# An fp32 attention and FFN layer on one core: other places for a few operations at the passage to Q and in front of O, and the low halves of the second half's x blocks moved from GpSimd to VectorE

## Chip, cores and metric

One core of a Trainium2 chip. The metric is the device time of one execution in microseconds; the lower the better.

## What is computed

```python
def reference(x, ctx, mask, Wq, Wk, Wv, Wo, W_base, b_base, W_router, A, B):
    # x, ctx: 16 x 128 x 1024, fp32; 32 query heads, 8 key/value heads of size 128
    q = rope(layernorm(x) @ Wq); k = rope(ctx @ Wk); v = ctx @ Wv
    s = 30 * tanh(q @ k.T * 0.0884 / 30); s = where(mask, s, -1e30)
    x = x + (softmax(s) @ v) @ Wo
    y = layernorm(x)
    w = softmax of the two largest of (y @ W_router.T), 0 for the others
    return x + y @ W_base.T + b_base + 2 * (((y @ A) * w) @ B)
```

## The kernel before

**Precision.** Every fp32 operand z is split in two: a high half (ScalarE copies z to an fp32r tile) and a low half (z less its high half, a subtraction on VectorE or GpSimd). `three` (L233 to L237) makes a product of two split operands from three matmuls, high x high, low x high and high x low, with 512 columns each. The work is in stages: K and V of the context, Q, attention with O, and the FFN.

**Stage Q** goes over 32 turns, 16 pairs of column blocks of Wq for each of two halves of the tokens. A turn n is seven products (Strassen's scheme, in Winograd's form), `QP` (L374), listed as (n, i) in the order i = 0, 1, 4, 3, 2, 5, 6; around turns 14 and 15 they are interleaved so that turn 15 lets go of the first half's x blocks early. The loops count products u = 0 to 223: product 102 is (15, 0), 112 is (16, 0), 113 (16, 1), 115 (16, 3), 117 (16, 5). Each product is 12 matmuls against one of seven x blocks `Xq[i]`. ScalarE (`act_q`) and VectorE (`dve_q`) run the same count. In step u VectorE does, in this order: `q_post` for product u - 1 (it adds products up in PSUM: L994, L998, L1003, L1006, L1009), `q_sum` (sums of Wq parts, L771 to L779), `q_low` of product u + 5 (L877), rope steps of finished turns (`TURN`, L387 to L401, 128x1024 each), and `x_low`, the low halves of an x block (L741). Product (n, 3) needs q_post(n, 1), and product (n, 5) needs q_post(n, 3). In turns 1 to 13 GpSimd does `q_low` for the raw parts of Wq.

**The x blocks of the first half** are loaded at the end of stage K/V. Blocks 5 and 6 are the last, loaded by SyncE when the last V product is done; ScalarE's `x_high` (L731) and VectorE's `x_low` of them stand in steps 1 and 2. **Those of the second half** are made by GpSimd in stage Q (`x_block`, L790): four rounds, round k starting at product XB + XB_STEP k with loads of `Bx`, adds and multiplications in steps 3 to 6 of the round, sums and stores to DRAM up to step 13. `x_load(1, i)` fetches block i once product (15, i) is done, `x_high` follows 4 steps after it, `x_low` in the same step, with the four parts k of a block shared out by `X_POOL` (L965): the listed ones on GpSimd, the others on VectorE. In all 18 parts are GpSimd's (4 + 3 + 3 + 3 + 3 + 2 + 0) and 10 are VectorE's.

**Attention and O** count steps `at` from -16 to 255 (`act_step` L1375, `dve_step` L1453, `pool_step` L1513, `pe_att` L1247). Up to step 0 TensorE still makes V of the last chunk (quarters at -16 to -10, then full products "full0" to "full2" and the last at -8, -6, -4, -2), among them the first scores and values: S0 to S10 stand for score products of the blocks x = 4 gi + b of group gi, PV0 and so on for products with V. For a score block: S on TensorE, tanh on ScalarE (L1387), min with the mask on VectorE (L1485), exp and its high half on ScalarE (L1407, L1409), its low half Pl on VectorE (L1498). For the sums of group gi: a product with ones, its copy `rT` (ScalarE L1401), a load of it into `r16` (GpSimd's queue, L1538), the reciprocal (VectorE L1502), a store to `rD` (L1521) and four loads of `RB` (L1531), both on GpSimd's queue; VectorE multiplies by RB (L1491), ScalarE makes the high half Ah (L1393), VectorE the low half Al (L1465). PV of block x needs Al of block x - 2. `v_high` (L1438), `v_low` (L1444) and `v_store` (GpSimd's queue, L1451, two stores of 256 KB each) take V out of PSUM; PV0 needs v_low(1), full1 needs v_low(0), PV1 needs v_low(4). `w_high` and `w_low` (L1215, L1220) split weights; 8 to 11 are the second half of Wv, which full0 reads, `SPLIT` (L1172) says at which step.

**The order of the work** is written by hand: tables give steps, each engine runs its steps in program order, and waits on semaphores do the rest. `Y` takes up O's products from PSUM: y_add (L1478), from the banks 3, 1, 0 in turn. `f_read` (L1847) says for what an FFN product waits before it writes a bank.

Of the kernel before, what the change touches and what calls it, by code (L numbers as in the profile page):

```python
# [97 lines left out]
def program(nc, xT, xN, ctxT, gran, mask, bias, cst, dram, out):  # L98
    kD, vD, vE, qD, XcD, QSD, X2D, x1D, rD = dram
    ctx = ExitStack()  # L100
    with ctx:
# [677 lines left out]
                e.tensor_tensor(S[:, 3, :], a12, S[:, 1, :], ALU.subtract).then_inc(*t.tick("q_sum", (n, 3)))  # L779


        XB, XB_STEP = 4, 23
        X_PART = {0: (0, 3), 1: (2, 5), 2: (4,), 3: (6, 1)}

        def x_stored(t):
# [176 lines left out]
                m.then_inc(*t.tick("q_pe", (n, i)))  # L962


        X_POOL = {0: (0, 1, 2, 3), 1: (0, 1, 2), 4: (0, 1, 2), 3: (0, 1, 2), 2: (0, 1, 2), 5: (0, 1), 6: ()}  # L965

        def act_q(t):
            e = t.e
            for u in range(NU + 1):
                if 0 < u and QP[u - 1][1] == 0:  # L970
                    n = QP[u - 1][0]
                    t.wait_ge("q_pe", (n, 0))
                    if n > 1:
                        for i in (4, 5, 6):
                            t.wait_ge("q_post", (n - 2, i))
                    e.activation(qp[n % 2][0][:, :], ps[qbank[n % 2][0]][:, :], ACT.Copy).then_inc(*t.tick("q_s1", n))
                if u + AHEAD < NU:
                    q_high(t, u + AHEAD)
                if u in (1, 2):
                    x_high(t, 0, 4 + u)  # L980
                if 0 <= u - 4 < NU and QP[u - 4][0] == 15:
                    x_high(t, 1, QP[u - 4][1])
                act_att_early(t, u)
# [57 lines left out]
        def dve_q(t):  # L1041
            for u in range(NU + 7):
# [6 lines left out]
                for x, ahead, i in ((0, 7, 1), (1, 6, 1), (2, 6, 3), (3, 7, 6)):  # L1049
                    if u + ahead < NU and 0 < QP[u + ahead][0] < 16 and QP[u + ahead][1] == i:  # L1050
                        q_sum(t, QP[u + ahead][0], x)
                if u + AHEAD < NU and not q_by_pool(u + AHEAD):
                    q_low(t, u + AHEAD)
                if u in (1, 2):
                    x_low(t, 0, 4 + u)
                for n, steps in TURN.get(u, []):
# [79 lines left out]
            x.sort()  # L1136
        PL_AT = {}
        for at, gi in DEN_AT.items():
            for b, d in enumerate((1, 2, 2, 2) if gi < 3 else (1, 2, 4, 6)):
                PL_AT.setdefault(at + d, []).append((gi, b))  # L1140
        NT = 8 * NG
        sbank, obank, tbank, ring = [4, 5], [2, 6], 7, [3, 1, 0]
# [232 lines left out]
        def act_step(t, at):  # L1375
            e = t.e
            if at == -16:
                q_high2(t, 0)
                q_high2(t, 1)
            v_high(t, at)  # L1380
            for x in SPLIT.get(at, []):
                w_high(t, x)
            for gi, b in S_AT.get(at, []):
                x = 4 * gi + b
                s = ps[sbank[x % 2]][:, :]
                t.wait_ge("a_s", x)
                e.activation(s, s, ACT.Tanh, scale=SCALE / CAP).then_inc(*t.tick("a_tanh", x))  # L1387
                q_high2(t, x + 2)
# [5 lines left out]
            if at in DEN_AT:  # L1394
                gi = DEN_AT[at]
                t.wait_ge("a_den", gi)
                if gi > 1:
                    t.wait_ge(f"d_rt{gi % 2}", gi - 2)
                else:
                    t.wait_ge("q_pe", (31, 4))  # L1400
                e.activation(rT[gi % 2][:, :], Tb[:, :], ACT.Copy).then_inc(*t.tick("a_rt", gi))  # L1401
            for gi, b in S_AT.get(at, []):
                x = 4 * gi + b
                s = ps[sbank[x % 2]][:, :]
                t.wait_ge("a_min", x)
                p_free(t, x)
                e.activation(Pf[x % NP][:, :], s, ACT.Exp, scale=CAP).then_inc(*t.tick("a_exp", x))  # L1407
                t.wait_ge("a_exp", x)
                e.activation(Ph[x % NP][:, :], Pf[x % NP][:, :], ACT.Copy).then_inc(*t.tick("a_ph", x))  # L1409
# [36 lines left out]
        def v_store(t, at):  # L1446
            for n in V_EVAC.get(at, []):
                half, b4 = n // 4, n % 4
                t.wait_ge("v_vl", n)
                for x in range(2):  # L1450
                    t.e.dma_start(vE[x, b4][:, T * half:T * half + T], f(v_place(n)[:, x, :])).then_inc(*t.tick(f"d_vp{n % 2}{x}", n, 16))  # L1451

        def dve_step(t, at):  # L1453
            e = t.e
            if at == -16:
                q_low2(t, 0)
                q_low2(t, 1)
            v_low(t, at)
            for gi, b in S_AT.get(at - 1, []):
                q_low2(t, 4 * gi + b + 2)  # L1460
            for gi, b in PV_AT.get(at - 1, []):
                x, i = 4 * gi + b, gi % 2
                t.wait_ge("a_ah", x)
# [2 lines left out]
            if at >= 9:  # L1466
# [9 lines left out]
                else:  # L1476
                    t.wait_ge("y_first", m)
                e.tensor_tensor(Y[:, m, :], ps[ring_bank(n)][:, :], Y[:, m, :], ALU.add).then_inc(*t.tick("y_add", n))  # L1478
            for x in [y for y in SPLIT.get(at, []) if at < 0]:
                w_low(t, x)  # L1480
            for gi, b in S_AT.get(at, []):
                x = 4 * gi + b
# [3 lines left out]
            for gi, b in PV_AT.get(at, []):  # L1486
# [2 lines left out]
                t.wait_ge("a_pv", x)  # L1489
                t.wait_ge(f"d_rb{b}", gi)  # L1490
                e.tensor_tensor(o, o, RB[:, b, :], ALU.mult).then_inc(*t.tick("a_an", x))  # L1491
            for x in [y for y in SPLIT.get(at, []) if at >= 0]:
                w_low(t, x)
            for gi, b in PL_AT.get(at, []):
                x = 4 * gi + b
                t.wait_ge("a_ph", x)
                t.wait_ge("a_den", gi)
                e.tensor_tensor(Pl[x % NP][:, :], Pf[x % NP][:, :], f(Ph[x % NP][:, :]), ALU.subtract).then_inc(*t.tick("a_pl", x))  # L1498
            if at - 1 in DEN_AT:
                gi = DEN_AT[at - 1]  # L1500
                t.wait_ge(f"d_rt{gi % 2}", gi)
                e.reciprocal(r16[gi % 2][:, :], r16[gi % 2][:, :]).then_inc(*t.tick("a_rec", gi))  # L1502
            if 11 <= at < 19:
                n = at - 11
                t.wait_ge("y_add", n + 8)
# [6 lines left out]

        def pool_step(t, at):  # L1513
            e = t.e
            if at - 2 in DEN_AT:
                gi = DEN_AT[at - 2]
                t.wait_ge("a_rec", gi)
                if gi > 1:
                    for b in range(4):
# [327 lines left out]
        def f_read(t, J):  # L1847

            if J < 0:
# [3 lines left out]
                elif bank in obank:  # L1853
                    t.wait_ge("a_al", 4 * NG - 1)
                else:
                    t.wait_ge("y_add", NT - 1)
                return
            c, m = J // 10, J % 10
            if m < 2:
# [371 lines left out]
```

## Time and profile before

| | |
|---|---|
| median of 3 runs | 2152.99 us (2149.18 to 2156.07) |
| profiled execution | 2150.67 us, span 2148.9 us |
| mean granted TensorE clock | 0.998 |
| busy: TensorE, VectorE, ScalarE, GpSimd | 2127.3, 1654.8, 878.0, 338.2 us |

Stage Q begins at 319.14 us of the span, attention at 937.08, the FFN at 1908.32. In the rows PE is TensorE, DVE VectorE, ACT ScalarE, POOL GpSimd, SP SyncE; a row of a timeline merges equal neighbours (x4), begins with start and duration in microseconds, and ends, where the engine was idle, with the idle time and what released it ("issue": nothing that the profile shows). A matmul's rows overlap, as the next one starts before the last has ended.

### The profile page before, as it was taken

The page shows a single profiled execution, that of the slowest core. Times are in us where ns is not written, and L with a number is a line of the kernel's source. Part 1 is how long each engine was busy: PE and PEld are TensorE (multiplying, and loading weights), DVE is VectorE, ACT ScalarE, POOL GpSimd, SP SyncE. Part 2 cuts the span into 40 slices and gives each one's busy share as a digit, 9 for nine tenths or more (in the row PEclk, how much of TensorE's full clock was granted, in tenths as well). Part 3 has the DMA queues.
Part 4 walks back from the last instruction along what each step waited for, and adds up shares of the span by engine and source line. Part 5 has one row for each costly group of instructions (what it writes and reads, how often), then busy time and mean ns, then how long its engine had stood idle before and what let it go on. Part 6 is the DMA issues. An engine that isn't in the chain of part 4 may idle for free.

```text
span 2148.9 us, 26502 instructions
## 1 busy us (share of the span) xinstructions
PE 2127.3 (99%) x9429; PEld 1723.2 (80%) x9429; DVE 1654.8 (77%) x2386; ACT 878.0 (41%) x1351; POOL 338.2 (16%) x437
## 2 busy tenths in 40 slices
PE   9999999999999999998999999999999999999999
PEld 7888887888888888876777777777877777888887
DVE  5969758898987666676887888988989898856533
ACT  3323343222241111145655556665666566423221
POOL 0000026555540000002111111111112110100000
PEclk9999999999999999999999999999999999999999
DMA  8778667777686665677755675678557864596761
GB/s 307 245 236 293 233 208 280 272 266 275 250 317 223 220 211 199 227 269 242 247 179 183 218 263 196 198 255 308 175 178 264 295 197 155 187 358 239 289 245 64
DMA packets 198531, 508.51 MB, mean 237 GB/s; under 512 B 20864, under 2 KB 46080, under 8 KB 196352
## 3 DMA queue, kind: packets, MB, share of 16 engines
q1 hardware_dynamic: 172160, 424.43, 56.3%
q0 software_dynamic: 26240, 82.38, 11.5%
q8 instruction: 76, 1.25, 0.2%
q14 instruction: 55, 0.45, 0.1%
HBM read 357.26 MB, written 149.16 MB: 236 GB/s over the span
## 4 chain that ended last, share of the span: by engine, by line
PE 93%; DMA 2%; DVE 2%; issue 2%; ACT 1%; SPq 0%; POOL 0%; ACTq 0%; DVEq 0%; POOLq 0%
PE pq L235 30%; PE pq L236 30%; PE pq L237 30%; PE pq L1290 1%; DMA kraw<-ctxT 1%; DMA QSD<-qW 0%; DMA RB<-rD 0%; DMA rD<-r 0%; PE pq L1891 0%; PE pq L1892 0%; DMA qD<-qt 0%; DVE Rl L1220 0%; DVE qW L877 0%; DVE Sq L774 0%; DVE Xq L741 0%
## 5 line engine op out<-in xcount | busy, mean ns | idle before, releaser
L235 PE MATMUL pq<-Ah,Rh 128*128 128x512 f32 x1024 | 399.6, 390 | 0.1
L236 PE MATMUL pq<-Al,Rh 128*128 128x512 f32 x1024 | 398.8, 389 | 0.0
L237 PE MATMUL pq<-Ah,Rl 128*128 128x512 f32 x1024 | 398.8, 389 | 0.0
L235 PE MATMUL pq<-Xq,qW 128*128 128x512 f32 x896 | 350.1, 391 | 5.1 <-issue 3.2
L236 PE MATMUL pq<-Xq,qW 128*128 128x512 f32 x896 | 349.3, 390 | 0.0
L237 PE MATMUL pq<-Xq,qW 128*128 128x512 f32 x896 | 349.2, 390 | 0.0
L1220 DVE TENSOR_TENSOR Rl<-raw,Rh 128x1024 fp32r<-128x1024 f32 x176 | 214.0, 1218 | 94.8 <-ACT Rh L1215 94.3
L1215 ACT ACTIVATE Rh<-raw 128x1024 fp32r<-128x1024 f32 x176 | 185.3, 1054 | 169.1 <-PE pq L237 131.3
L235 PEld LDWEIGHTS pq<-Ah,Rh 128*128 128x128 f32 x1024 | 192.5, 188 | 43.5 <-ACT Y L1414 2.1
L237 PEld LDWEIGHTS pq<-Ah,Rl 128*128 128x128 f32 x1024 | 192.4, 188 | 40.4
L236 PEld LDWEIGHTS pq<-Al,Rh 128*128 128x128 f32 x1024 | 192.4, 188 | 40.0
L235 PEld LDWEIGHTS pq<-Xq,qW 128*128 128x128 f32 x896 | 168.6, 188 | 43.3 <-issue 7.1
L237 PEld LDWEIGHTS pq<-Xq,qW 128*128 128x128 f32 x896 | 168.6, 188 | 35.0
L236 PEld LDWEIGHTS pq<-Xq,qW 128*128 128x128 f32 x896 | 168.6, 188 | 34.6
L1478 DVE TENSOR_TENSOR Y<-pq,Y 128x512 f32<-128x512 f32 x248 | 169.3, 683 | 30.9 <-PE pq L237 30.6
L864 ACT ACTIVATE qW<-qraw 128x512 fp32r<-128x512 f32 x96 | 60.6, 632 | 295.6 <-PE pq L237 268.6
L1387 ACT ACTIVATE pq<-pq 128x512 f32<-128x512 f32 x128 | 74.6, 583 | 208.9 <-PE pq L237 208.7
L1538 POOL DMA_DIRECT2D r<-rT x32 | 22.9, 716 | 753.2 <-ACT rT L1401 734.6
L1485 DVE TENSOR_TENSOR pq<-pq,Bm 128x512 f32<-128x512 f32 x128 | 88.8, 694 | 65.4 <-ACT pq L1387 64.6
L1393 ACT ACTIVATE Ah<-pq 128x512 fp32r<-128x512 f32 x128 | 76.6, 598 | 99.7 <-DVE pq L1491 99.5
L235 PE MATMUL pq<-F,Rh 128*128 128x512 f32 x288 | 112.9, 392 | 0.0
L237 PE MATMUL pq<-F,Rl 128*128 128x512 f32 x288 | 112.2, 390 | 0.0
(243 smaller groups left out, 3942.0 us busy)
## 6 DMA issues: line engine op xcount, KB each, us to landing
raw<-gran SPq DMA_DIRECT2D x177, 512.0 KB, 4.4
QSD<-qW SPq DMA_DIRECT2D x64, 512.0 KB, 3.5
qD<-qt SPq DMA_DIRECT2D x128, 256.0 KB, 5.5
qW<-QSD SPq DMA_DIRECT2D x64, 512.0 KB, 3.5
qf<-qD SPq DMA_DIRECT2D x64, 512.0 KB, 6.1
RB<-rD POOLq DMA_DIRECT2D x128, 256.0 KB, 4.3
qraw<-gran SPq DMA_DIRECT2D x48, 512.0 KB, 5.0
kD<-kst SPq DMA_DIRECT2D x32, 512.0 KB, 5.6
```

Source lines behind the costliest of these rows:

```text
L235: e.matmul(dst, lh, rh, start=first, stop=False, skip_group_check=more)
L236: e.matmul(dst, lh, rl, start=False, stop=False, skip_group_check=more)
L237: return e.matmul(dst, ll, rh, start=False, stop=last, skip_group_check=more)
L864: e.activation(q_place(u)[:, 0, :], q_source(u), ACT.Copy).then_inc(*t.tick("q_hi", u))
L1215: t.e.activation(piece(x)[1], raw[raw_of(x)][:, :], ACT.Copy).then_inc(*t.tick("w_hi", x))
L1220: t.e.tensor_tensor(l, raw[raw_of(x)][:, :], f(h), ALU.subtract).then_inc(*t.tick("w_lo", x))
L1290: m = e.matmul(Tb[32 * y:32 * y + 32, :], f(ones[:, 0:32]), Pf[(4 * gi + y) % NP][:, :], start=True, stop=True, tile_position=(0, 32 * y))
L1387: e.activation(s, s, ACT.Tanh, scale=SCALE / CAP).then_inc(*t.tick("a_tanh", x))
L1393: e.activation(Ah[:, 4 * i:4 * i + 4, b * P:b * P + P], v4(ps[obank[x % 2]][:, :]), ACT.Copy).then_inc(*t.tick("a_ah", x))
L1478: e.tensor_tensor(Y[:, m, :], ps[ring_bank(n)][:, :], Y[:, m, :], ALU.add).then_inc(*t.tick("y_add", n))
L1485: e.tensor_tensor(v4(s), v4(s), bc(Bm[:, :].unsqueeze(1), [P, 4, P]), ALU.min).then_inc(*t.tick("a_min", x))
L1538: e.dma_start(r16[gi % 2][:, :], rT[gi % 2][0:P:32, :]).then_inc(*t.tick(f"d_rt{gi % 2}", gi, 16))
```

## The change

Six edits. `x_block` starts at product 9 and every 22 products, instead of 4 and 23. `X_POOL` is empty, so that VectorE makes all low halves of the second half's blocks. At the passage to Q ScalarE makes the high halves of blocks 5 and 6 in step 1, ahead of q_high(7), and VectorE makes q_low(8) in step 4, behind the q_posts, instead of step 3. In front of O: w_high(11) and w_low(11) go ahead of v_high and v_low of 0 and 1, the reciprocal of group 0 ahead of that v_low (and its store to rD from GpSimd's step -8 to -9, ahead of the four v_stores), v_high(4) ahead of an exp, w_low(8) to w_low(10) behind the min of their step. The low halves Pl of groups 1 and 2 are spread over more steps. And the first FFN product of each bank waits for the last y_add that read this bank, instead of the last of all.

```diff
@@ -779,7 +779,7 @@
                 e.tensor_tensor(S[:, 3, :], a12, S[:, 1, :], ALU.subtract).then_inc(*t.tick("q_sum", (n, 3)))
 
 
-        XB, XB_STEP = 4, 23
+        XB, XB_STEP = 9, 22
         X_PART = {0: (0, 3), 1: (2, 5), 2: (4,), 3: (6, 1)}
 
         def x_stored(t):
@@ -962,7 +962,7 @@
                 m.then_inc(*t.tick("q_pe", (n, i)))
 
 
-        X_POOL = {0: (0, 1, 2, 3), 1: (0, 1, 2), 4: (0, 1, 2), 3: (0, 1, 2), 2: (0, 1, 2), 5: (0, 1), 6: ()}
+        X_POOL = {i: () for i in range(7)}
 
         def act_q(t):
             e = t.e
@@ -976,8 +976,9 @@
                     e.activation(qp[n % 2][0][:, :], ps[qbank[n % 2][0]][:, :], ACT.Copy).then_inc(*t.tick("q_s1", n))
                 if u + AHEAD < NU:
                     q_high(t, u + AHEAD)
-                if u in (1, 2):
-                    x_high(t, 0, 4 + u)
+                if u == 1:
+                    x_high(t, 0, 5)
+                    x_high(t, 0, 6)
                 if 0 <= u - 4 < NU and QP[u - 4][0] == 15:
                     x_high(t, 1, QP[u - 4][1])
                 act_att_early(t, u)
@@ -1049,8 +1050,9 @@
                 for x, ahead, i in ((0, 7, 1), (1, 6, 1), (2, 6, 3), (3, 7, 6)):
                     if u + ahead < NU and 0 < QP[u + ahead][0] < 16 and QP[u + ahead][1] == i:
                         q_sum(t, QP[u + ahead][0], x)
-                if u + AHEAD < NU and not q_by_pool(u + AHEAD):
-                    q_low(t, u + AHEAD)
+                for w in {3: (), 4: (3 + AHEAD, 4 + AHEAD)}.get(u, (u + AHEAD,)):
+                    if w < NU and not q_by_pool(w):
+                        q_low(t, w)
                 if u in (1, 2):
                     x_low(t, 0, 4 + u)
                 for n, steps in TURN.get(u, []):
@@ -1136,7 +1138,7 @@
             x.sort()
         PL_AT = {}
         for at, gi in DEN_AT.items():
-            for b, d in enumerate((1, 2, 2, 2) if gi < 3 else (1, 2, 4, 6)):
+            for b, d in enumerate({0: (1, 2, 2, 2), 1: (1, 2, 3, 4), 2: (1, 3, 4, 6)}.get(gi, (1, 2, 4, 6))):
                 PL_AT.setdefault(at + d, []).append((gi, b))
         NT = 8 * NG
         sbank, obank, tbank, ring = [4, 5], [2, 6], 7, [3, 1, 0]
@@ -1377,9 +1379,12 @@
             if at == -16:
                 q_high2(t, 0)
                 q_high2(t, 1)
-            v_high(t, at)
+            if at not in (-9, -6):
+                v_high(t, at)
             for x in SPLIT.get(at, []):
                 w_high(t, x)
+            if at == -9:
+                v_high(t, at)
             for gi, b in S_AT.get(at, []):
                 x = 4 * gi + b
                 s = ps[sbank[x % 2]][:, :]
@@ -1399,6 +1404,8 @@
                 else:
                     t.wait_ge("q_pe", (31, 4))
                 e.activation(rT[gi % 2][:, :], Tb[:, :], ACT.Copy).then_inc(*t.tick("a_rt", gi))
+            if at == -7:
+                v_high(t, -6)
             for gi, b in S_AT.get(at, []):
                 x = 4 * gi + b
                 s = ps[sbank[x % 2]][:, :]
@@ -1450,14 +1457,23 @@
                 for x in range(2):
                     t.e.dma_start(vE[x, b4][:, T * half:T * half + T], f(v_place(n)[:, x, :])).then_inc(*t.tick(f"d_vp{n % 2}{x}", n, 16))
 
+        def row_sums(t, gi):
+            t.wait_ge(f"d_rt{gi % 2}", gi)
+            t.e.reciprocal(r16[gi % 2][:, :], r16[gi % 2][:, :]).then_inc(*t.tick("a_rec", gi))
+
         def dve_step(t, at):
             e = t.e
             if at == -16:
                 q_low2(t, 0)
                 q_low2(t, 1)
-            v_low(t, at)
+            if at != -9:
+                v_low(t, at)
             for gi, b in S_AT.get(at - 1, []):
                 q_low2(t, 4 * gi + b + 2)
+            if at == -9:
+                w_low(t, 11)
+                row_sums(t, 0)
+                v_low(t, at)
             for gi, b in PV_AT.get(at - 1, []):
                 x, i = 4 * gi + b, gi % 2
                 t.wait_ge("a_ah", x)
@@ -1476,7 +1492,7 @@
                 else:
                     t.wait_ge("y_first", m)
                 e.tensor_tensor(Y[:, m, :], ps[ring_bank(n)][:, :], Y[:, m, :], ALU.add).then_inc(*t.tick("y_add", n))
-            for x in [y for y in SPLIT.get(at, []) if at < 0]:
+            for x in [y for y in SPLIT.get(at, []) if at < 0 and y not in (11,) + (8, 9, 10)]:
                 w_low(t, x)
             for gi, b in S_AT.get(at, []):
                 x = 4 * gi + b
@@ -1489,17 +1505,15 @@
                 t.wait_ge("a_pv", x)
                 t.wait_ge(f"d_rb{b}", gi)
                 e.tensor_tensor(o, o, RB[:, b, :], ALU.mult).then_inc(*t.tick("a_an", x))
-            for x in [y for y in SPLIT.get(at, []) if at >= 0]:
+            for x in [y for y in SPLIT.get(at, []) if at >= 0 or y in (8, 9, 10)]:
                 w_low(t, x)
             for gi, b in PL_AT.get(at, []):
                 x = 4 * gi + b
                 t.wait_ge("a_ph", x)
                 t.wait_ge("a_den", gi)
                 e.tensor_tensor(Pl[x % NP][:, :], Pf[x % NP][:, :], f(Ph[x % NP][:, :]), ALU.subtract).then_inc(*t.tick("a_pl", x))
-            if at - 1 in DEN_AT:
-                gi = DEN_AT[at - 1]
-                t.wait_ge(f"d_rt{gi % 2}", gi)
-                e.reciprocal(r16[gi % 2][:, :], r16[gi % 2][:, :]).then_inc(*t.tick("a_rec", gi))
+            if at - 1 in DEN_AT and at != -9:
+                row_sums(t, DEN_AT[at - 1])
             if 11 <= at < 19:
                 n = at - 11
                 t.wait_ge("y_add", n + 8)
@@ -1512,8 +1526,8 @@
 
         def pool_step(t, at):
             e = t.e
-            if at - 2 in DEN_AT:
-                gi = DEN_AT[at - 2]
+            if at - 2 in DEN_AT and at != -8 or at == -9:
+                gi = DEN_AT[-10 if at == -9 else at - 2]
                 t.wait_ge("a_rec", gi)
                 if gi > 1:
                     for b in range(4):
@@ -1853,7 +1867,7 @@
                 elif bank in obank:
                     t.wait_ge("a_al", 4 * NG - 1)
                 else:
-                    t.wait_ge("y_add", NT - 1)
+                    t.wait_ge("y_add", max(n for n in range(NT - 3, NT) if ring_bank(n) == bank))
                 return
             c, m = J // 10, J % 10
             if m < 2:
```

## Rows read from the trace of the kernel before

**Rows 1.** The page of the profiled execution: busy us (share of the span) x instructions.

```profile
PE 2127.3 (99%) x9429; PEld 1723.2 (80%) x9429; DVE 1654.8 (77%) x2386; ACT 878.0 (41%) x1351; POOL 338.2 (16%) x437
```

**Rows 2.** Timeline of TensorE, passage to Q; last, a window's busy times, granted clock, DMA share, GB/s.

```profile
319.14 0.39 PE L235 MATMUL pq<-Xq,qW 128*128 128x512 f32 x1
...
327.07 0.39 PE L237 MATMUL pq<-Xq,qW 128*128 128x512 f32 x1
329.67 0.77 PE L235 MATMUL pq<-Xq,qW 128*128 128x512 f32 x1 [2.21 <-issue]
...
333.12 0.40 PE L237 MATMUL pq<-Xq,qW 128*128 128x512 f32 x1
...
337.71 0.47 PE L235 MATMUL pq<-Xq,qW 128*128 128x512 f32 x1 [0.76 <-DVE qW L877]
...
330.00:340.00 10.00, 9.24 (x34) 7.16 (x34) 6.80 (x11) 4.39 (x8) 3.42 (x5) 0.85 0.93 351
```

**Rows 3.** Timelines of ScalarE and VectorE in the same stretch.

```profile
332.05 0.63 ACT L864 ACTIVATE qW<-qraw 128x512 fp32r<-128x512 f32 x1 [3.88 <-DMA QSD<-qW]
...
327.68 1.29 DVE L741 TENSOR_TENSOR Xq<-Xq 128x512 fp32r<-128x512 f32 x2 [1.11 <-ACT Xq L731]
328.89 0.68 DVE L994 TENSOR_TENSOR qp<-pq,qp 128x512 f32<-128x512 f32 x1
...
333.23 3.17 DVE L741 TENSOR_TENSOR Xq<-Xq 128x512 fp32r<-128x512 f32 x4 [3.06 <-ACT Xq L731]
...
336.93 0.68 DVE L998 TENSOR_TENSOR qp<-pq,qp 128x512 f32<-128x512 f32 x1
```

**Rows 4.** Timelines of TensorE and VectorE beside GpSimd's first and fourth x block.

```profile
370.23 0.39 PE L237 MATMUL pq<-Xq,qW 128*128 128x512 f32 x1
370.62 0.47 PE L235 MATMUL pq<-Xq,qW 128*128 128x512 f32 x1
...
568.23 0.47 PE L235 MATMUL pq<-Xq,qW 128*128 128x512 f32 x1 [1.17 <-DVE qp L998]
...
561.15 3.47 DVE L774 TENSOR_TENSOR Sq<-Sq,qraw 128x512 f32<-128x512 f32 x1
```

**Rows 5.** Timeline of VectorE where the second half begins.

```profile
623.22 1.42 DVE L741 TENSOR_TENSOR Xq<-Xq 128x512 fp32r<-128x512 f32 x1
...
628.14 1.21 DVE L398 TENSOR_TENSOR qt<-pq,qt 128x1024 f32<-128x1024 f32 x1
...
638.92 0.68 DVE L994 TENSOR_TENSOR qp<-pq,qp 128x512 f32<-128x512 f32 x1
...
647.63 2.48 DVE L741 TENSOR_TENSOR Xq<-Xq 128x512 fp32r<-128x512 f32 x4
```

**Rows 6.** Timeline of TensorE there: first matmuls of products 115 and 117.

```profile
639.70 0.47 PE L235 MATMUL pq<-Xq,qW 128*128 128x512 f32 x1 [0.40 <-issue]
...
645.95 0.47 PE L235 MATMUL pq<-Xq,qW 128*128 128x512 f32 x1 [0.57 <-issue]
```

**Rows 7.** Timeline of TensorE in front of O: full0 at w_low(11), then PV2.

```profile
972.25 0.50 PE L235 MATMUL pq<-Rh,Vh 128*128 128x512 f32 x1 [1.61 <-DVE Rl L1220]
...
983.93 0.47 PE L235 MATMUL pq<-Ph,vT 128*128 128x512 f32 x1 [2.00 <-DVE Al L1465]
```

**Rows 8.** Timelines of GpSimd and VectorE there; landing times of r/rD, then of RB.

```profile
967.81 0.72 POOL L1538 DMA_DIRECT2D r<-rT  x1 [322.54 <-ACT rT L1401]
...
973.24 0.25 DVE L1502 RECIPROCAL r<-r 128x16 f32<-128x16 f32 x1 [0.44 <-DMA r<-rT]
...
981.74 0.70 DVE L1491 TENSOR_TENSOR pq<-pq,RB 128x512 f32<-128x512 f32 x1 [0.28 <-DMA RB<-rD]
...
DMA to landing us min/median/max: 2.1/3.3/5.4
...
DMA to landing us min/median/max: 3.5/6.9/7.8
```

**Rows 9.** Timeline of TensorE: the first matmul of the FFN.

```profile
1908.32 0.50 PE L1891 MATMUL pq<-F,Rh 128*128 128x512 f32 x1 [0.78 <-DVE Y L1478]
```

## The prediction

> **What bounds the kernel now.** I read the page first: TensorE is busy for 99% of the span [rows 1]. So the time is the matmuls plus the moments when TensorE waits, and all waits, the first matmul's and the tail's included, come to 2148.9 less 2127.3, some 22 us. A change that only reorders other engines' work can win no more than that. Then I read TensorE's timeline for its pitch and its gaps. From product 0 of stage Q to the last matmul of product 2 there are 35 pitches in 7.93 us [rows 2], 0.2266 us each, so a product of 12 matmuls takes 2.72 us. A matmul's row lasts 0.39 us, 0.16 more than the pitch, so a wait costs the idle time in brackets plus 0.16. A longer wait costs twice: after the one of 2.37 us in rows 2 the next 8 pitches take 3.45 us (329.67 to 333.12) instead of 1.81, with the matmul at 0.77 us at first: the granted clock is 0.85 on average from 330 to 340 [rows 2], so it has been at the lower of its two levels, 1.2 GHz, for a while. That is 1.64 us more. After the wait of 1.77 us at 972.25 [rows 7] it stayed at the upper one. The price of a fall is therefore 1.6 us, and it comes somewhere between 1.8 and 2.2 us of wait.
>
> With that, the waits that the change can reach are these: at the passage to Q 2.37 + 1.64, and 0.92 at 337.71 [rows 2]; 1.3 at 568.23 and 0.2 at 370.62 (0.39 us behind the matmul before), beside blocks that GpSimd makes [rows 4]; 0.56 and 0.73 where the second half begins [rows 6]; 1.77 and 2.16 + 1.6 before O [rows 7], with a smaller one of S3; 0.94 at the first FFN product [rows 9].
>
> **Passage to Q.** The long wait is product 3's. It needs q_post(0,1), and rows 3 show why that is late: VectorE works in order, and the low halves of block 5 (327.68, two of them) stand ahead of the q_post at 328.89. They wait for block 5's load. The diff leaves x_low(5) ahead of q_post(0,1), and the load where it is, so I cost this at no gain: 4.0 us stay. The wait at 337.71 is another. Block 6's high halves stood behind q_high(7), which ScalarE could only do at 332.05, so its low halves ran from 333.23 to 336.4, then q_low(8), and q_post(0,3), needed by product 5, came at 336.93 [rows 3]. Now block 6 goes ahead of q_high(7), and q_low(8) behind q_post(0,3). Product 3 ends at 329.67 + 2.72 + 1.64 = 334.0, the q_post can follow at once, and product 5 finds it done: **-0.9**. If block 6's load lands late this is 0. q_high(7), behind block 6 now, has room: it waits for a store until 332.05 anyhow, and product 7 is 10 us off.
>
> **GpSimd's x blocks.** The blocks' adds begin 3 products after XB + 22k instead of XB + 23k: at products 12, 34, 56, 78, before 7, 30, 53, 76. One turn of Wq is 7 products, so in the turn they stood at 0, 2, 4, 6 and now stand at 5, 6, 0, 1. VectorE's adds with both inputs in SBUF take 0.68 us alone and up to 3.47 beside GpSimd's [rows 4]; the block at phase 6 made a q_post late and cost TensorE 1.3, phase 0 cost 0.2, phases 2 and 4 nothing. Phases 6 and 0 stay, moved to other blocks. Phases 5 and 1 are new; each lies between 0 and 1.6, the worst of these rows rounded up. I take 0.3 each, nearer to their cheap neighbours: **+0.6**, bounds -1.5 (all waits go) and +3.2. The later end (product 91 against 89) is covered: x_stored is asked for at product 97. Loads and stores go with their blocks, no more of them.
>
> **All low halves on VectorE.** 18 subtractions leave GpSimd. Here I count VectorE's queue, in the loop's order, up to q_post(16,1), which product 115 needs. It started at 638.92 and product 115 was 0.56 late with it [rows 5, 6]: VectorE had no slack. From 623.22, where block 1's low halves stand, the queue becomes: 4 low halves of block 1; q_post 3 and 4; four rope steps; 4 of block 4; q_post, q_low, q_post, q_low; a rope step; 4 of block 3; a rope step; 4 of block 2; q_post(16,1). The low halves go at 0.60 each (four in 2.48 at 647.63 [rows 5]), rope steps at 1.14 (1.22 less overlap, row 628.14), q_posts 0.6 to 0.7. So 16 x 0.605 + 1.32 + 4 x 1.135 + 4 x 0.60 + 1.14 + 1.14 + 0.68 = 20.9, less nothing for waits, since ScalarE's high halves are earlier than each of these. q_post(16,1) ends at 644.1 and product 115 starts at 644.2, 4.5 later than now. The release of GpSimd's grip is in this already: I use 0.60 for every low half, where the one at 623.22 took 1.42. The wait becomes 5.1 us, so the clock falls: +1.6. Behind it VectorE has caught up (product 117's q_post ends at 650, product 117 starts at 651.3), and the 0.73 us there goes. **4.5 + 1.6 - 0.7 = +5.4.** Bounds: +3.8 without the fall, +7.0 if the lower clock lasts twice as long, as no row here shows a wait this long.
>
> The Trainium skill (SBUF — State Buffer, "Who interferes with whom") says that a VectorE tensor_tensor with both inputs in SBUF and a GpSimd read of SBUF exclude each other for a whole instruction, and the later one blocks. The stretched rows agree [rows 4, 5], while rope steps, with an input in PSUM, keep 1.22. That rule speaks for this edit.
>
> **Before O.** (a) Low halves 8 to 10 go behind the min: VectorE's sum up to q_low2(3), which S3 needs too, is the same, so S3's wait stays. (b) w_low(11) goes ahead of v_low(0,1): the 1.77 at 972.25 shrinks to some 0.4. (c) But row_sums(0), which waits for the r load (issued 967.81, the reciprocal 973.24 waited for it [rows 8]), now stands ahead of v_low(0), v_low(1) and the Pl that PV0 needs: 0.2 + 1.2 + 0.7 behind the landing. With r landing at 972.5 (between the median 3.3 and the maximum 5.4 of rows 8) PV0 starts at 974.7; now it starts 9 matmuls after 972.25, near 974.4. So (b) is turned into a wait for PV0, net +0.3. PV1 comes 27 matmuls later, 980.8, and its wait for v_low(4) is gone with v_high(4) done a step earlier. (d) PV2 waits for the chain reciprocal, rD, RB, 981.74 [rows 8], Ah, Al: 8.5 us from the start of the reciprocal to the first product with RB. The reciprocal is 0.7 earlier, but the four stores of v_low(0,1), formerly issued before it, now go to GpSimd's queue between rD and RB. I let these cancel: PV2 stays at 983.9, **0.0**. Bounds: -0.7 and r at the median, -0.6, and no fall of the clock, -1.6, make -2.9; RB landing in 6.9 us instead of 3.5 [rows 8], +3.4 - 0.7, makes +2.7. The stores themselves come some 3 us later; nothing in this stretch reads them. SyncE's raw loads behind w_low(8) to (10) come up to 1.2 us later, for weights that are split 10 us on: 0. (e) The Pl of groups 1 and 2 spread out: VectorE has gaps of microseconds at RB there; 0.
>
> **FFN.** The first product waits for the last y_add though its bank was read two adds earlier. Now it waits for that one, done before the last O product ends: **-0.9** [rows 9]. TensorE runs on from there to the end, so it arrives.
>
> **Sum:** -0.9 + 0.6 + 5.4 + 0.0 - 0.9 = +4.2. The profiled execution took 2150.67 (span 2148.9), which would be 2154.9; it stands 2.3 below the median of the runs, 2152.99, so against that the forecast is **2157.2**.
>
> **Rivals.** *VectorE keeps up* where the second half begins: freed of GpSimd, it gains more than I give it, both waits of rows 6 go, -1.3 instead of +5.4, and the sum is -2.5: 2150.5. For it: a subtraction beside GpSimd took 1.42 instead of 0.60 [rows 5], and an add 3.47 [rows 4]. Against it: 12 more subtractions before product 115 are 7.3 us, which nine such stretches would have to pay. Chance 0.20. The exclusion that the Trainium skill (SBUF — State Buffer, "Who interferes with whom") states is the reason why there could be so many.
> *RB late:* RB(0) queues behind the four stores. Place: PV2. Price: up to 3.4 - 0.7 = 2.7, so +6.9, 2159.9. It decides from 2.3 us on. For it: the median landing is 6.9; against it: SyncE loads little just then. 0.12.
> *The long wait at the passage goes too,* if block 5's load lands sooner without the early Bx loads: -4.0, so +0.2, 2153.2. Against it: those are issued after it. 0.05.
> The forecast 0.55; the rest, 0.08, is phases 5 and 1 costing or saving 2 us more.
>
> **Numbers.** 0.3% (6.5 us) is what a measurement can tell here. Forecast case: 0.49 within, 0.06 slower. VectorE keeps up: 0.14 within, 0.06 faster. RB late: 0.12 slower. Passage: 0.05 within. Rest: 0.04 each side. Together faster 0.10, same 0.68, slower 0.22. The forecast's own range is 2153 to 2161. The range given runs from the first rival less 2.5 for the clock and the phases, 2148, to RB late with a bad phase, 2163.
>
> **What would show it.** TensorE's gap at 337.71 gone, the one at 329.67 there; a wait of some 5 us near product 115, released by VectorE's q_post, with 0.77 us matmuls behind it; no GpSimd subtraction after 600; PV0 waiting for Pl; no gap at the first FFN product. If product 115 starts on time, the main term is wrong.

## The result, and the profile after

The changed kernel ran in 2154.86 us (median of 22 runs, 2151.08 to 2162.59) beside 2149.77 for the kernel before (22 runs): a ratio of 1.0024 [1.0016, 1.0033], slower by 5.1 us. The forecast was +4.2, 2157.2. The profiled executions differ by 3.4 us. Three executions, one each of both_back, phase_two and the kernel before beside them, took 3045 to 4343 us in the slow state and are left out of every median and ratio.

First the page, to set beside [rows 1]: GpSimd gave 18 instructions to VectorE and is 25.6 us less busy. TensorE's busy time cannot show a wait.

```profile
span 2152.3 us, 26503 instructions
PE 2128.7 (99%) x9429; PEld 1724.3 (80%) x9429; DVE 1663.4 (77%) x2404; ACT 878.9 (41%) x1351; POOL 312.6 (15%) x419
```

Then TensorE's timeline, at the same places as [rows 2, 4, 6]:

```profile
326.66 0.39 PE L237 MATMUL pq<-Xq,qW 128*128 128x512 f32 x1
329.50 0.47 PE L235 MATMUL pq<-Xq,qW 128*128 128x512 f32 x1 [2.45 <-issue]
388.18 0.47 PE L235 MATMUL pq<-Xq,qW 128*128 128x512 f32 x1 [1.28 <-DVE qp L995]
452.36 0.47 PE L235 MATMUL pq<-Xq,qW 128*128 128x512 f32 x1 [1.14 <-DVE qp L999]
568.39 0.47 PE L235 MATMUL pq<-Xq,qW 128*128 128x512 f32 x1 [1.10 <-DVE qp L999]
626.62 0.47 PE L235 MATMUL pq<-Xq,qW 128*128 128x512 f32 x1 [0.84 <-DVE qp L999]
644.31 0.47 PE L235 MATMUL pq<-Xq,qW 128*128 128x512 f32 x1 [3.82 <-issue]
645.89 0.63 PE L237 MATMUL pq<-Xq,qW 128*128 128x512 f32 x1
```

With 0.16 added to the idle time in brackets, these are the waits. (Figures of a wait below are always such a sum, or the excess of a start-to-start distance over 0.2265, the pitch.) The products that wait are, in order, 3, 24, 47, 89, 110 and 115. The wait for product 3 is there (2.6), that for product 5 is not. Three waits of 1.26 to 1.44 stand in the stretch of GpSimd's rounds, where before there was one of this size. At 626.62 product 110 waits 1.0, and at 644.31 product 115 waits 4.0, with matmuls at the lower clock behind it; "issue" stands for VectorE's q_post(16,1), which ends at 644.2. Here is VectorE's queue ahead of both:

```profile
623.39 2.49 DVE L741 TENSOR_TENSOR Xq<-Xq 128x512 fp32r<-128x512 f32 x4
625.79 0.69 DVE L999 TENSOR_TENSOR qp<-pq,qp 128x512 f32<-128x512 f32 x1
631.64 2.49 DVE L741 TENSOR_TENSOR Xq<-Xq 128x512 fp32r<-128x512 f32 x4
637.57 2.50 DVE L741 TENSOR_TENSOR Xq<-Xq 128x512 fp32r<-128x512 f32 x4
639.98 1.23 DVE L389 TENSOR_TENSOR qt<-pq,cs 128x1024 f32<-128x1024 f32 x1
641.11 2.50 DVE L741 TENSOR_TENSOR Xq<-Xq 128x512 fp32r<-128x512 f32 x4
643.51 0.70 DVE L995 TENSOR_TENSOR qp<-pq,qp 128x512 f32<-128x512 f32 x1
```

Before O and at the FFN, beside [rows 7 to 9]; the last row is the first FFN matmul, one pitch behind the one ahead:

```profile
976.51 0.50 PE L235 MATMUL pq<-Rh,Vh 128*128 128x512 f32 x1 [0.28 <-DVE Rl L1222]
979.37 0.47 PE L235 MATMUL pq<-Ph,vT 128*128 128x512 f32 x1 [0.50 <-DVE Pl L1514]
988.61 0.47 PE L235 MATMUL pq<-Ph,vT 128*128 128x512 f32 x1 [2.18 <-DVE Al L1481]
1911.68 0.39 PE L237 MATMUL pq<-Ah,Rl 128*128 128x512 f32 x1
1911.90 0.39 PE L1905 MATMUL pq<-F,Rh 128*128 128x512 f32 x1
```

GpSimd's queue and VectorE's rows for the same chain:

```profile
973.41 0.72 POOL L1552 DMA_DIRECT2D r<-rT  x1 [397.23 <-ACT rT L1406]
977.83 0.55 POOL L1535 DMA_DIRECT2D rD<-r  x1 [3.70 <-DVE r L1462]
978.37 2.15 POOL L1458 DMA_DIRECT2D vE<-Ah  x4
982.65 1.08 POOL L1545 DMA_DIRECT2D RB<-rD  x2 [2.12 <-DMA rD<-r]
```
```profile
977.28 0.25 DVE L1462 RECIPROCAL r<-r 128x16 f32<-128x16 f32 x1 [0.82 <-DMA r<-rT]
986.41 0.70 DVE L1507 TENSOR_TENSOR pq<-pq,RB 128x512 f32<-128x512 f32 x1 [1.03 <-DMA RB<-rD]
```

rD's write is issued first now, and four stores between it and RB: 4.8 us from its issue to RB's (977.83 to 982.65) instead of 4.2.

By stages the two profiles differ so: Q up to attention's first wait 629.51 us (319.14 to 948.65) against 635.51 (318.73 to 954.24), **+6.0**; from there to the first FFN matmul 959.7 against 957.7, **-2.0**; what lies before Q and in the FFN -0.6.

### The profile page after: what moved, and what is told of

Same layout as the page of the kernel before. It is cut to its first block, busy times and chain, and to the rows that moved or that the text cites. A ratio compares the mean times of both kernels' runs of the same rounds, so it can differ in the third digit from the quotient of the medians.

```text
span 2152.3 us, 26503 instructions
## 1 busy us (share of the span) xinstructions
PE 2128.7 (99%) x9429; PEld 1724.3 (80%) x9429; DVE 1663.4 (77%) x2404; ACT 878.9 (41%) x1351; POOL 312.6 (15%) x419
## 4 chain that ended last, share of the span: by engine, by line
PE 93%; DVE 3%; DMA 2%; issue 1%; ACT 0%; SPq 0%; POOL 0%; DVEq 0%; ACTq 0%; POOLq 0%
PE pq L235 30%; PE pq L236 30%; PE pq L237 30%; PE pq L1292 1%; DMA RB<-rD 1%; DMA kraw<-ctxT 0%; DVE qW L877 0%; DMA rD<-r 0%; DVE Sq L774 0%; PE pq L1906 0%; PE pq L1905 0%; DMA qD<-qt 0%; DVE pq L395 0%; DVE qt L389 0%; DMA r<-rT 0%
```

## The experiments

Each row is the median of 5 or more runs, with its ratio to the kernel before on the same chip. The kernels ran on three chips, on which the kernel before took 2149.98 to 2152.09 us, so kernels are compared by their ratios. A ratio of 0.001 is 2.15 us.

| kernel | from | us | ratio |
|---|---|---|---|
| halves_back | after | 2151.49 | 1.0008 [0.9996, 1.0021] |
| rounds_back | after | 2152.37 | 1.0015 [1.0004, 1.0026] |
| both_back (the orders alone) | after | 2147.31 | 0.9984 [0.9974, 0.9993] |
| halves_alone | before | 2156.33 | 1.0035 [1.0022, 1.0047] |
| post_first | before | 2154.70 | 1.0016 [1.0003, 1.0028] |
| late_halves | after | 2155.80 | 1.0027 [1.0016, 1.0037] |
| passage_open | both_back | 2147.05 | 0.9988 [0.9978, 0.9997] |
| phase_two | before | 2147.37 | 0.9989 [0.9977, 1.0000] |
| phase_orders | passage_open | 2142.74 | 0.9965 [0.9952, 0.9979] |
| phase_orders_lag | phase_orders | 2141.74 | 0.9958 [0.9945, 0.9972] |
| stores_behind | after | 2152.47 | 1.0012 [1.0001, 1.0022] |
| all_together | the last two | 2138.63 | 0.9944 [0.9929, 0.9958] |

### Which part costs

**halves_back:** the low halves as before, all else changed.

```diff
-X_POOL = {i: () for i in range(7)}
+X_POOL = {0: (0, 1, 2, 3), 1: (0, 1, 2), 4: (0, 1, 2), 3: (0, 1, 2), 2: (0, 1, 2), 5: (0, 1), 6: ()}
```

> The changed kernel with the old X_POOL, so that 18 low halves are GpSimd's again; all else as changed. Theory (VectorE's queue): TensorE's wait of 4.0 us before product 115, the 1.0 us one before product 110 and the 1.6 us of lower clock behind them go, and the old 0.56 and 0.73 come back: 5.3 us less than the changed kernel. Rival (GpSimd's release of VectorE pays for the added work, and the waits come from elsewhere, the block loads say): the waits stay, and the time is that of the changed kernel or above it.

2151.49 us. The waits of 1.0 and 4.0 are gone, and the two of before are back, as the theory had it:

```profile
639.27 0.47 PE L235 MATMUL pq<-Xq,qW 128*128 128x512 f32 x1 [0.40 <-issue]
645.52 0.47 PE L235 MATMUL pq<-Xq,qW 128*128 128x512 f32 x1 [0.53 <-issue]
```

**rounds_back:** `XB, XB_STEP = 4, 23` in the changed kernel.

> The changed kernel with XB, XB_STEP = 4, 23 again. Theory (the phase of GpSimd's rounds in the turn of 7 products sets what VectorE loses): TensorE's waits between product 12 and 95 are those of the kernel before, some 0.4 us at phase 0, none at 2 and 4, 1.3 at phase 6, in all 2.0 instead of 4.3; 2.3 us less than the changed kernel. Rival (the four waits come from the other edits, the passage's order say): they stay at 4.3.

2152.37 us. One wait is left in the stretch of the rounds, 1.33 in front of product 89 (567.26), and the 4.0 at product 115 stays.

**both_back:** the two edits together; only the orders remain of the change.

> The changed kernel with the old X_POOL and XB, XB_STEP = 4, 23: the orders at the passage, in front of O and before the FFN alone. Theory (the sum of parts): no wait of the 5 us kind where the second half begins (0.56 and 0.7 there), one of 1.3 at phase 6, none at the FFN: 0 to 3 us below the kernel before, by whether the clock falls at the passage. Rival (the orders in front of O cost what the rest gains): the time of the kernel before or above it, and PV2's wait the larger for it.

2147.31 us, and the gaps at product 5 and at the FFN stay closed. Product 3 waits 2.0, and product 10 another 2.1 with a clock fall behind it (passage_open below shows why). And the round of phase 6 cost 4.65 and a clock fall this time, where it cost 1.3 in rounds_back, which has the same rounds: the same collision comes at different prices. These are the matmul that waits, and VectorE and GpSimd ahead of it:

```profile
564.67 0.72 PE L235 MATMUL pq<-Xq,qW 128*128 128x512 f32 x1 [4.49 <-DVE qp L995]
```
```profile
555.88 3.55 DVE L771 TENSOR_TENSOR Sq<-qraw 128x512 f32<-128x512 f32 x1
559.35 3.44 DVE L877 TENSOR_TENSOR qW<-Sq,qW 128x512 fp32r<-128x512 f32 x1
```
```profile
556.33 1.30 POOL L877 TENSOR_TENSOR qW<-qraw,qW 128x512 fp32r<-128x512 f32 x1
```

Two operations of 0.68 each took 3.5 here; in rounds_back the same two took 0.68 and 1.77.

**halves_alone:** only `X_POOL = {i: () ...}` in the kernel before.

> The kernel before with only X_POOL emptied. Theory (VectorE's queue): waits of 1.0, about 4 us and 1.6 of lower clock where the second half begins, 1.3 saved, 5.3 us above the kernel before. Rival (the damage needs the other edits too): less than 2 us above it.

2156.33 us, the slowest of all, with 1.0 at product 110 and 3.99 + 1.56 at 115. By the ratios the low halves cost 7.5 us alone, 6.7 beside the orders (rounds_back against both_back) and 3.4 beside orders and new rounds (the changed kernel against halves_back). Each ratio is uncertain by 2 to 3 us, and the difference of two by about 3 to 3.5, so all three figures allow the 5.3 that the profiles show, and they do not show that the other edits change the cost of the low halves.

### The passage to Q

**post_first:** in the kernel before, block 5's low halves go behind q_post(0,1).

```diff
-                if u in (1, 2):
-                    x_low(t, 0, 4 + u)
+                if u == 2:
+                    x_low(t, 0, 5)
+                    x_low(t, 0, 6)
```

> The kernel before with both low halves of blocks 5 and 6 in step 2, behind q_post(0,1), where block 5's stood in step 1 ahead of it. Theory (the long wait at the passage is the q_post behind block 5's low halves in VectorE's queue, not the block's load itself): the wait of 2.4 us before product 3 goes, with any fall of the clock behind it; product 5 may wait up to 1 us as before. 2.4 us below the kernel before, 4.0 where the clock fell. Rival (block 5's load bounds the passage whatever the order): the wait moves to product 5, and the time stays.

Product 3's wait was gone, but product 5 waited instead, and the 4 us were not won: block 6's high halves still stood behind q_high(7). That is the sign that the rival named, but not its cause: block 5's low halves were done at 328.3, and those of block 6 kept product 5 waiting. (Another 6.2 us went in the rounds, at the old phase 6.)

```profile
336.44 0.77 PE L235 MATMUL pq<-Xq,qW 128*128 128x512 f32 x1 [4.58 <-DVE qW L877]
```
```profile
331.98 3.15 DVE L741 TENSOR_TENSOR Xq<-Xq 128x512 fp32r<-128x512 f32 x4 [3.71 <-ACT Xq L731]
335.06 0.68 DVE L877 TENSOR_TENSOR qW<-Sq,qW 128x512 fp32r<-128x512 f32 x1
335.66 0.68 DVE L998 TENSOR_TENSOR qp<-pq,qp 128x512 f32<-128x512 f32 x1
```

**passage_open:** both_back, with block 5's low halves in step 2 (behind q_post(0,1)) and block 6's in step 4 (behind the q_posts, ahead of q_low(8)).

```diff
-                if u in (1, 2):
-                    x_low(t, 0, 4 + u)
+                if u == 4:
+                    x_low(t, 0, 6)
+                for w in {3: (), 4: (3 + AHEAD, 4 + AHEAD)}.get(u, (u + AHEAD,)):
...
+                if u == 2:
+                    x_low(t, 0, 5)
```

> both_back with block 5's low halves in step 2 behind q_post(0,1), and block 6's in step 4 behind q_post(0,3) and ahead of q_low(8). Theory (the passage's waits are q_posts behind low halves; in post_first the first one only moved on to product 5, whose q_post stood behind block 6): products 0 to 6 run without a wait above 0.3 us, 2.6 us less than both_back, 4 where its clock fell. Rival (the loads of blocks 5 and 6 bound the passage): product 5 or 6 waits 2 us or more for its x block.

No matmul waits from 318 to 345 us. But product 10 waits 3.9 and the clock falls. VectorE idled for a load of Wq's parts, which q_sum needs, and q_post(1,1) stood behind it:

```profile
349.12 0.76 PE L235 MATMUL pq<-Xq,qW 128*128 128x512 f32 x1 [3.72 <-DVE qp L995]
```
```profile
344.21 1.36 DVE L771 TENSOR_TENSOR Sq<-qraw 128x512 f32<-128x512 f32 x1 [2.47 <-DMA qraw<-gran]
345.50 1.75 DVE L877 TENSOR_TENSOR qW<-Sq,qW 128x512 fp32r<-128x512 f32 x1
347.16 1.21 DVE L389 TENSOR_TENSOR qt<-pq,cs 128x1024 f32<-128x1024 f32 x1
348.30 0.68 DVE L995 TENSOR_TENSOR qp<-pq,qp 128x512 f32<-128x512 f32 x1
```

In both_back, too, VectorE waited for this load, 3.85 us, and product 10 for VectorE; in the kernel before it did not. So part of the long wait of [rows 2] had hidden this load. q_low in the second of these rows takes 1.75 instead of 0.68, beside GpSimd's round that starts at product 4. The theory was right on products 0 to 6, but the 2.6 to 4 us were not won: the ratio is no better than both_back's.

### Too much work, or its order

**late_halves:** the changed kernel, with blocks 1 and 2 one step and block 5 two steps later, and turn 15's rope in two steps of three (the lines of the rope are left out below).

```diff
...
-((0, 4), (1, 4), (4, 4), (3, 4), (2, 4), (5, 4), (6, 5))
+((0, 4), (1, 5), (4, 4), (3, 4), (2, 5), (5, 6), (6, 5))
```

> The changed kernel, all low halves on VectorE, but in the order of need: block 1's one step later, block 2's behind q_post(16,1), block 5's behind q_post(16,3), and turn 15's six rope steps last, in steps 117 and 118. Theory (too much work for VectorE before product 119, not only its order): the wait at product 115 falls below 0.7 us, and one of 3 to 5 us appears at product 119, which needs the rope of turn 15; time within 2 us of the changed kernel. Rival (the order alone): no wait above 1 us from product 108 to 124, 5 us less than the changed kernel.

The wait moved to product 119 and grew, and the time stayed:

```profile
655.93 0.77 PE L235 MATMUL pq<-Xq,qW 128*128 128x512 f32 x1 [5.11 <-DVE qt L398]
```

With all low halves VectorE has too much work between 623 and 655 us, in both orders tried.

### The rounds

**phase_two:** the kernel before with `XB, XB_STEP = 6, 21`, so that every round starts at phase 6 and its adds three products later, at phase 2.

> The kernel before with XB, XB_STEP = 6, 21, so that all four rounds of x blocks stand at phase 2 in the turn. Theory (the phase decides): no wait above 0.2 us between product 12 and 95; 1.6 us less than the kernel before, 2.0 with the small ones. Rival (the overlap of GpSimd's and VectorE's instructions is set by details that shift from one run or turn to the next): waits of 0.5 to 4 us in one or more rounds in spite of it.

No wait above 0.1 us from 341 to 636 us, 2147.37 us, as the theory had it. At the passage, which this edit leaves alone, product 3 waited 2.4 and product 5 another 2.3, with the clock fall behind the second.

**phase_orders:** passage_open with these rounds.

> The order of the passage at which products 0 to 6 did not wait, the changed order in front of O, x-block low halves on GpSimd as before, and GpSimd's x-block rounds all in phase 2 of 7 (steps 6, 27, 48, 69). Theory (the waits at products 0 to 6 were an order, and those of the rounds a collision at a wrong phase): no wait between 319 and 636 us but at most one below 1 us, then 0.6 and 0.7 us at products 115 and 116, about 6 us of waits between 945 and 990 us and no wait ahead of the feed-forward part. Against the kernel before, 5 to 7 us of the 320-640 us stretch go (4.0 at the passage, 2.0 in the rounds) and 0.9 ahead of the feed-forward part: 2144 to 2146 us, ratio 0.997 to 0.998. Rival (VectorE at the passage has one block's work too many, so that a wait cured at one product comes back at a later one): no wait at products 0 to 6 but 3 to 5 us and a clock fall at products 8 to 12, as in the run with the rounds at phase 4, and 2147 to 2149 us.

2142.74 us, 1.3 under the range expected. Again there is no wait in the rounds, and product 10 waits 2.2, more than the theory allowed, without a clock fall. With the first round two products later, q_sum's load was still what VectorE waited for (2.56 us at 343.02).

**phase_orders_lag:** in phase_orders, x block 2 one step later and block 5 two.

```diff
-((0, 4), (1, 4), (4, 4), (3, 4), (2, 4), (5, 4), (6, 5))
+((0, 4), (1, 4), (4, 4), (3, 4), (2, 5), (5, 6), (6, 5))
```

> phase_orders with the low halves of x block 2 of the second half one step later and those of block 5 two steps later. Theory (with GpSimd taking its share, VectorE is only momentarily behind at products 115 and 116, so that spreading its work helps where it did not in the changed kernel): the waits of 0.6 and 0.7 us there go, and the time is 1 to 1.3 us under phase_orders. Rival (the work of this stretch is too much for VectorE in any order): the wait moves to a product up to four places later and is 1 us or more, and the time is that of phase_orders or up to 1 us more.

Of 0.56 and 0.68 there remains 0.29 in the profile. The medians differ by 1.0 us, within their intervals, so the gain is shown by the profile alone.

### Before O

**stores_behind:** in the changed kernel, the four stores of step -9 behind RB(0)'s loads.

```diff
-            v_store(t, at)
+            if at == -8:
+                v_store(t, -9)
+            if at != -9:
+                v_store(t, at)
```

> The changed kernel, with the four stores of V's first two half tiles (step -9) issued on GpSimd's queue behind the four loads of RB(0) instead of between rD's write and them. Theory (those four stores share the DMA queues with rD's write and with RB(0) and make each later): rD's write lands in 3.8 us as before instead of 4.8, RB(0) follows in 3.5 to 3.8, RB's first product comes 12.5 to 13.0 us behind rT instead of 13.9, and the wait at PV product 2 falls from 2.3 to about 1.2 us; the time falls by 1 us, to a ratio of 1.002 against the kernel before. Rival (the landing of rD's write varies by itself, and the stores cost nothing): rD's write takes 4.5 us or more again, and the wait at PV product 2 stays at 2 to 2.6 us.

rD's write to RB's issue took 3.75 (4.82 in the changed kernel), RB's first product came at 984.24, and PV2 waits 1.2 instead of 2.3, with no fall behind it. In the rows of GpSimd below the stores of L1458 stand no more between rD and RB.

```profile
976.68 0.55 POOL L1535 DMA_DIRECT2D rD<-r  x1 [2.80 <-DVE r L1462]
980.43 2.16 POOL L1545 DMA_DIRECT2D RB<-rD  x4 [3.20 <-DMA rD<-r]
```
```profile
986.43 0.47 PE L235 MATMUL pq<-Ph,vT 128*128 128x512 f32 x1 [1.02 <-DVE Al L1481]
```

Against the changed kernel's profile alone this proves little, because r also landed 0.9 sooner there. Nor does rD's landing alone: with the stores behind it, rD's write to RB's issue took from 3.7 to 4.8 in eight profiles, so it does vary by itself, as the rival has it. But over all profiles from the issue of rD's write to the first product with RB it is 7.8 to 9.0 us in the eight with the stores between, and 7.5 and 7.6 in the two without. PV2 waits 1.5 to 2.7 in the eight, and 1.2 and 1.1 in the two. From attention's first wait to the first FFN matmul it is 954.7 to 957.7 in the eight, and 952.5 and 952.6 in the two. By these profiles, clock falls included, the stores' place is worth 2 us or more, where the theory gave it 1; the ratio went from 1.0024 to 1.0012, 2.6 us, with an uncertainty as large.

**all_together:** this edit in phase_orders_lag.

> phase_orders_lag and stores_behind in one kernel. Theory (the effects add: each is a wait of TensorE at its own place): no wait above 0.5 us between 319 and 940 us but the one at product 10 (2.1 us), a wait at PV product 2 of at most 1.2 us instead of 2.7 and no clock fall there, and 1 to 1.5 us under phase_orders_lag, 2140 to 2141 us, ratio 0.995 to 0.996 against the kernel before. Rival (RB's product has waited behind VectorE's own queue, so that earlier loads of RB change nothing in this kernel): the wait at PV product 2 stays at 1.5 us or more, and the time is that of phase_orders_lag, 2141 to 2142.5 us.

2138.63 us, under both kernels and 1.4 under the range expected. PV2 waits 1.1 (975.37, 0.93 idle), product 10 2.0. The median is 13.5 us under that of the kernel before, and the ratio says 0.6% [0.4, 0.7].

## Why the prediction was right, and where not

It called for +4.2, within the 0.3% that it gave as the bound of what can be told; the runs show +5.1, or 0.24%, and the profile +3.4. The main term holds, mechanism and size. The sum is better than its other terms:

- **All low halves on VectorE, +5.4: right in size.** Counted in the loop's order, VectorE's queue was to end at 644.1; it ended at 644.2. The waits are 1.0 + 4.0 + 1.6 of clock less 1.3, +5.3. What the count missed is product 110: block 1's low halves (623.39) also stand ahead of q_post(15,3). It costs no more in sum, as TensorE arrives 1.0 later at 115. halves_back has 5.3 less there in the profile, 3.4 less by the ratios. The rival, that VectorE freed of GpSimd keeps up, is out: its low halves did take 0.60 each, and 12 more ahead of product 115 are still too many.
- **Rounds, +0.6: the step that failed.** "I take 0.3 each, nearer to their cheap neighbours", the prediction says of phases 5 and 1. In the profile they cost 1.44 and 1.26, phases 6 and 0 1.3 and 0.2: 4.2 in all against 1.5 before. With the small delays behind each wait, products 12 to 97 take 2.9 longer, inside the bound of +3.2. The ratios give +1.9 (against rounds_back) and +5.2 (halves_back against both_back), each uncertain by about 3. Four profiles have the new rounds (after, halves_back, late_halves, stores_behind): phases 1 and 6 cost 1.3 in each, phase 5 cost 1.4, nothing, 1.4 and 1.7, and phase 0 cost 0.2, 0.9, 0.9 and 0.2. Nor was the base firm: with the old rounds the stretch cost 1.3 to 1.5 in four profiles and 6.2 in two. Phase 2, which the prediction had found free, was free in all four runs that used it alone. (The phase is that of a round's first adds; the waits come 10 to 13 products later, beside its last sums. Why one phase costs and another does not was not taken apart.) Ahead of product 24 the cause is in view, VectorE first and then GpSimd:

```profile
382.65 3.65 DVE L877 TENSOR_TENSOR qW<-Sq,qW 128x512 fp32r<-128x512 f32 x1 [0.66 <-ACT qW L864]
386.22 1.21 DVE L389 TENSOR_TENSOR qt<-pq,cs 128x1024 f32<-128x1024 f32 x1
387.36 0.67 DVE L995 TENSOR_TENSOR qp<-pq,qp 128x512 f32<-128x512 f32 x1
```
```profile
381.96 2.54 POOL L877 TENSOR_TENSOR qW<-qraw,qW 128x512 fp32r<-128x512 f32 x2
384.45 1.28 POOL L826 TENSOR_TENSOR Bx<-Bx,Bx 128x512 f32<-128x512 f32 x1
```

  A subtraction of 0.68 lasts until GpSimd pauses, at 385.73, and 0.6 more: 3.65. This is what the Trainium skill (SBUF — State Buffer, "Who interferes with whom") says of two such inputs, that the later one blocks, and the trace agrees, but for two things. The subtraction waited for more than one instruction, through the boundary at 384.45. And in both_back VectorE's add at 555.88 took 3.55 although GpSimd's next operation began only at 556.33, so the earlier one was held too. (A slip without effect: the last stores of the rounds are in steps 88 and 86, not 91 and 89.)
- **Passage, -0.9: right on the wait, too small by the other profiles.** q_post(0,3) came at 332.54 and product 5 did not wait, for the reason given. The 4.0 were to stay; of them 2.6 did, because the clock did not fall in this profile (-1.4). This is partly luck: in rounds_back, which has the same order there, the wait is 3.75 and the clock falls. But the 0.92 of product 5 was luck as well: in halves_alone and phase_two, with the old order, product 5 waits 2.2 and 2.3, and the clock falls behind it. In all, products 0 to 7 lose 5.1, 6.5 and 6.5 us in the three profiles with the old order (before, halves_alone, phase_two). In the six with the new one they lose 2.1 to 3.0 in five and 5.5 in rounds_back, and both_back, one of the five, loses 3.8 more at product 10. So the order probably gains more than 0.9, and no run has it alone.
- **Before O, 0.0: -0.9.** From attention's first wait to PV2 there are 35.3 us before (948.65 to 983.93) and 34.4 after (954.24 to 988.61). What failed is the landing of r. The prediction put it at 972.5 in the kernel before; but [rows 8] show the reciprocal at 973.24 waiting for it, 5.4 us from its issue, so its place in VectorE's queue alone could not make it sooner. It came sooner because r landed sooner, in 3.9. That is hardly chance: in the four profiles with the old order r took 5.3 to 7.3 from issue to reciprocal, in the ten with the new one 3.0 to 4.8. In the old order the four stores of V follow r's load on GpSimd's queue, in the new one rD's write; that they held r up fits this, but no run tests it alone. PV0 waits 0.67, as foreseen, and PV1's 0.46, named but given no price, is gone. The stores now cost between rD and RB what the prediction let cancel: 0.6 on the chain in this profile (9.1 against 8.5). The rival "RB late" had the right place and too high a price. From attention's first wait to the FFN the four profiles with the old order take 957.6 to 963.3, the eight with the new one 954.7 to 957.7. The means differ by 4.8 us, the FFN's 0.9 in it; the pair of profiles compared here differs by only 2.0.
- **FFN, -0.9: right** (0.94 before, none now).

In the profile, -0.9 - 1.4 + 2.9 + 5.3 - 0.9 - 0.9 are +4.1, and with the -0.6 before Q and in the FFN +3.5, for 3.4 measured. A term that was too low (rounds) and two that were too high (the passage, before O) nearly cancelled, so the total's fit is partly luck. Why the medians differ by 1.7 us more than the two profiles is open. both_back says that the orders alone gain 3.4 us [1.5, 5.6], where the prediction's terms for them come to 1.8.

## What to carry to other kernels

Count the queue of the engine that takes over work, instruction by instruction, up to each operation that another engine waits for, the early ones too: that count was good to 0.1 us. Price a change of phase between two engines by the phase that the trace shows free, and take the others at the worst seen, not between; even that was passed once the same phase cost 4.65 and a fall. A wait removed brings TensorE sooner to the next load: look there first.

## What was not expected of the hardware

Whether the clock falls behind a wait of about 2 to 3 us varies from run to run. Waits of 2.0 (stores_behind), 2.4 (halves_back, PV2), 2.6 (rounds_back, PV2), 2.7 (halves_back, product 3) and 2.9 (late_halves, product 3) kept the granted clock at 2.4 GHz. Waits of 2.0 (all_together, product 10), 2.2 and 2.4 (before), 2.5 (late_halves, PV2) and 2.7 (phase_orders_lag, PV2) were followed by eight or so matmuls at 1.2 GHz, 1.4 to 1.6 us. In phase_two a wait of 2.3 at PV1 kept the clock, and one of 1.8 at PV2, 2.6 us later, was followed by a fall that cost 2.6 us. All waits of 3.75 and more were followed by a fall, which cost 1.4 to 2.6. The prediction took a bound between 1.8 and 2.2 from two waits; there is none so sharp. Stretches of 10 us, granted clock in the last but two column:

```profile
640.00:650.00 10.00, 6.18 (x21) 4.61 (x20) 10.00 (x15) 4.40 (x8) 0.00 (x0) 0.83 0.73 282
330.00:340.00 10.00, 10.00 (x45) 8.25 (x44) 7.57 (x12) 4.35 (x8) 2.76 (x2) 1.00 0.84 292
```

The first follows product 115's wait, the second product 3's, in one execution of the changed kernel. So a term for the clock behind a wait of 2 to 3 us is a chance times 1.6, and a difference of 1.6 us between two profiles is not evidence.
